# Four of the first seven context loads issued by ScalarE, two small tables loaded later, and another order of the last unit's products

## The chip, the cores and the metric

The kernel runs on one core of a Trainium2 chip. The metric is the time of one execution on the device, in microseconds (us). The engines are TensorE (PE, with its weight loads as PEld), VectorE (DVE), ScalarE (ACT), GpSimd (POOL) and SyncE (SP), which here only issues transfers. Each has its own list of instructions and waits on semaphores that the others raise. 16 DMA engines move the data. In the profile q1 is the queue of SyncE, q10 that of ScalarE, q0 that of GpSimd.

## The reference

Two layers on x (2 batches x 64 positions x 1024) with a context of 2 x 1024 x 1024. Only the very first step matters here, a matmul of x and the context, both rounded to 8-bit codes:

```python
q1 = fake_quant(x1, x1_scale, x1_zp)      # x1 = layernorm(x)
q2 = fake_quant(x2, x2_scale, x2_zp)      # x2 = ctx_4096
...
    q = jnp.clip(jnp.round(x / s + z), QMIN, QMAX)
    return (q - z) * s
...
x = x + jnp.matmul(q1, q2)
x = x + mamba_layer(layernorm(x))         # first product: hidden @ W_in.T
```

Then come a state space layer (`W_in`, convolution, scan, `W_out`), a routed low-rank layer, cross attention on the context, self attention and a small MLP.

## The kernel before

The weights and the context are cut into units of 128 partitions x 2048 float32 (1 MiB, 8 KB per partition). `units` lists them in the order of use: units 0 to 7 are the context, 8 to 23 `w_in`, and so on. They go through a ring of 7 slots; `place(n)` is the slot of unit n, `unit_in[slot]` its semaphore (16 per transfer). SyncE issues x, then all units in order (L516, L533). Unit 7 takes the slot of unit 0 and is issued when unit 0 is coded (`ctx_scaled`, 1), unit 8 when unit 1 is coded. Ahead of unit 12 stand five small loads of the state space layer, `a_par` the last of them.

The context stage, with who does what:
- ScalarE (L675) turns each unit into 8-bit codes as soon as it has landed, 0 to 7 in order; unit 7 in two halves. Between units 1 and 2 it also sums the codes of x (L670).
- VectorE normalizes x, codes it (`q1`), then for each unit takes off 128 and writes bf16 (L1453, `ctx_coded`). Between units 0 and 1 it copies the transposed q1 (L1458), which TensorE's products need.
- TensorE transposes q1 (L931), then for each unit makes four products with q1 (L956) and four with ones (L957, the sums that the zero point needs), in turns. Units 0 to 3 are the first 512 columns of x, 4 to 7 the second. For the second half of unit 7 it waits for `ctx_coded`, 9. After units 3 and 7 it raises `q_done`. Then come 17 idle products (34 matmuls of the trace, L937), which only keep it busy, and the transposes of the next h.
- VectorE, after its last code, adds offset (L1464) and product (L1469) of each half to x, each followed by the statistics for the next layernorm (L1413). GpSimd takes the variance to the power of -0.5 (L558). Then h is written (L1422), transposed, copied by ScalarE and VectorE (L686, L1495), and the products with `w_in` begin (L1017).

At its start GpSimd issues `tables` (72 KB, L546; read first in the self attention near the end) and ScalarE issues `quant` (the four scales, L658) and `tri` (32 KB, L659; read by the routing after the state space layer). After its second variance root GpSimd waits for `q_done`, 2, and clears the edge of `uT` (L587), which VectorE needs before it copies the first projection (L1501). In the scan of the state space layer ScalarE makes 256 exponentials (L768) for 32 steps; at step 26 it issues five loads (L815 to L819).

Of the kernel before, what the change touches and what calls it, by code (L numbers as in the profile page):

```python
# [21 lines left out]
P = 128  # L22
B, L = 2, 64
D = 1024
KT = D // P
UK = 4
UN = 512
UNIT = UK * UN
SPARE = 2
SLOTS = 7  # L30
LN_EPS = 1e-5

# [56 lines left out]
def perceiver(nc, dram, out):  # L89
    units = unit_list()  # L90
# [6 lines left out]
    with ExitStack() as stack:  # L97
# [5 lines left out]

        ring = sb("ring", [P, SLOTS, UNIT])
        x = sb("x", [P, D])
# [3 lines left out]
        small = sb("small", [P, 640])  # L109
# [9 lines left out]
        psum = stack.enter_context(nc.psum_tensor("psum", [P, 8, 512], F32))  # L119
# [54 lines left out]
        tri = carve(small, 528, NE, NE)  # L174


        q2 = arena[:, 0:8192].bitcast(BF16).rearrange("p (u n) -> p u n", u=8)
        q1T = arena[:, 8192:8704].bitcast(BF16).rearrange("p (k t) -> p k t", k=KT)
# [43 lines left out]
        ring_more = carve(arena, 7168, UNIT)  # L222
        ring_spare = carve(arena, 11392, SPARE, UNIT)

# [29 lines left out]

        unit_in = [sem(f"unit_in{s}") for s in range(SLOTS + 2)]
        x_in = sem("x_in")
        quant_in = sem("quant_in")
        tables_in = sem("tables_in")
        tri_in = sem("tri_in")
# [38 lines left out]
        q_done = sem("q_done")  # L298
# [150 lines left out]

        spare = range(first["ctx_again"], first["ctx_again"] + SPARE)  # L450
        before_spare = split_done[sum(n < spare[0] for n in split_units) - 1]
        turns = []
        slot_of = []
# [7 lines left out]
        def place(n):  # L461
            if slot_of[n] > SLOTS:
                return ring_spare[:, slot_of[n] - SLOTS - 1, :]
            return ring_more if slot_of[n] == SLOTS else ring[:, slot_of[n], :]
# [8 lines left out]
        def arrived(eng, n):  # L473
            if n in spare:

                eng.wait_ge(unit_in[SLOTS + 1], 16 * SPARE)
            else:
# [36 lines left out]
        @block.sync  # L514
        def _(sp):
            sp.dma_start(x[:, :], dram["x"]).then_inc(x_in, 16)  # L516
            for n, (name, i) in enumerate(units):
                if n == 12:

                    sp.dma_start(small[:, 320:416], dram["chan"]).then_inc(mamba_in, 16)  # L520
                    sp.dma_start(rms_w, dram["rms_w"].to_broadcast([P, SSM])).then_inc(mamba_in, 16)
                    sp.dma_start(wxT, dram["wx"]).then_inc(mamba_in, 16)
                    sp.dma_start(wdtT[0:R + 1, :], dram["wdt"]).then_inc(mamba_in, 16)
                    sp.dma_start(a_par, dram["a_par"]).then_inc(mamba_in, 16)

                if n == more:
                    sp.wait_ge(y_psum, 2)
                elif n in spare:

                    sp.wait_ge(*before_spare)  # L530
                elif n >= SLOTS:
                    sp.wait_ge(*last_use[before(n)])
                sp.dma_start(place(n), dram[name][i]).then_inc(unit_in[min(slot_of[n], SLOTS + 1)], 16)  # L533

            sp.wait_ge(v_ready, 3)
            sp.dma_start(vdup[L:P, 0, :], vdup[0:L, 0, :]).then_inc(vdup_in, 16)
            sp.dma_start(vdup[0:L, 1, :], vdup[L:P, 1, :]).then_inc(vdup_in, 16)
            for nh in range(2):
                sp.wait_ge(y_ready, nh + 1)
                cols = slice(nh * UN, nh * UN + UN)  # L540
                sp.dma_start(out[:, cols], y_out[:, cols]).then_inc(out_done, 16)
            sp.wait_ge(out_done, 32)

        @block.gpsimd
        def _(pool):
            pool.dma_start(small[:, 160:304], dram["tables"]).then_inc(tables_in, 16)  # L546
            pool.memset(ident[:, :], 0.0).then_inc(const_zero, 1)
            pool.memset(minus_half, -0.5).then_inc(const_zero, 1)
            pool.memset(const_warm, 0.0).then_inc(const_ready, 1)
# [33 lines left out]

            rstd_of(1)

            pool.wait_ge(q_done, 2)
            pool.memset(uT[:, :, :, 0:CK - 1], 0.0).then_inc(edge_zero, 1)  # L587

            pool.wait_ge(ssm_sum, 1)
# [59 lines left out]
        def _(act):  # L649
# [6 lines left out]


            act.dma_start(quant, dram["quant"].to_broadcast([P, 4])).then_inc(quant_in, 16)  # L658
            act.dma_start(tri, dram["tri"]).then_inc(tri_in, 16)  # L659

            act.wait_ge(const_ready, 3)
            step(act.activation(const_warm, const_warm, ACT.Identity))
# [132 lines left out]
            for s in range(3, STEPS):  # L797
                decay(s)
                if s - 1 in Z_AT:
                    softplus_exp(2 + Z_AT.index(s - 1))  # L800
                    softplus_log(2 + Z_AT.index(s - 1))
                if s - 1 in DU_AT:
                    du_copy(DU_AT.index(s - 1) + 1)
                if s == 17:
                    proj_copy(6)
                if s - 1 in GATE_AT:
                    gate_tanh(GATE_AT.index(s - 1))
                if s == 29:
                    proj_copy(7)
                if s == 30:  # L810
                    gated_high(GATE_HALF)
                if s == 26:

                    act.wait_ge(du_copied, NG)
                    act.dma_start(lora_b, dram["lora_b"]).then_inc(rank_in, 16)  # L815
                    act.dma_start(w_ar, dram["w_ar"]).then_inc(rank_in, 16)
                    act.dma_start(b_base, dram["b_base"]).then_inc(bias_in, 16)
                    act.dma_start(bq, dram["bq"].to_broadcast([P, D])).then_inc(bias_in, 16)
                    act.dma_start(bk, dram["bk"].to_broadcast([P, D])).then_inc(bias_in, 16)  # L819
# [61 lines left out]
            for r in range(GQ):  # L881
                last = act.activation(krep[:, :, r, :], krot.rearrange("p (g d) -> p g d", g=HKV), ACT.Copy)
# [3 lines left out]
            for b in range(B):  # L886
                rows = slice(L * b, L * b + L)
# [38 lines left out]
        def _(pe):  # L926
# [17 lines left out]
            for nh in range(2):  # L944
                for kh in range(2):
                    for b in range(B):
                        u = 4 * nh + 2 * kh + b
                        pe.wait_ge(ctx_coded, u + 1)
                        rows = slice(L * b, L * b + L)
                        for k in range(UK):  # L950
                            if u == 7 and k == UK // 2:
                                pe.wait_ge(ctx_coded, 9)
                            right = q2[:, u, UN * k:UN * k + UN]
                            at = dict(start=(kh == 0 and k == 0), stop=(kh == 1 and k == UK - 1))

                            pe.matmul(psum[rows, nh, :], q1T[:, UK * kh + k, rows], right, **at)  # L956
                            last = pe.matmul(psum[rows, 2 + nh, :], ones64, right, **at)  # L957
                last.then_inc(q_done, 1)

            def split_products(bank, left, m, k0, start, stop, signal, hook=None, fresh=None):  # L960

# [233 lines left out]
            for k in range(KT):  # L1195
                last = pe.matmul(psum[:, 2, 0:NE * RANK + NE], hT[:, k, :], w_ar[:, k, :], start=(k == 0), stop=(k == KT - 1))
# [159 lines left out]
            for nh in range(2):  # L1356
                for part, signal in enumerate((hs_high, hs_low)):
                    for k in range(KT):
                        if nh == 0 and k % 4 == 0:
                            pe.wait_ge(signal, 9 + k // 4)  # L1360
                        last = pe.matmul(psum[:, 4 + nh, :], split[:, part, k, :], onehot[:, k, UN * nh:UN * nh + UN],  # L1361
                                         start=(part == 0 and k == 0), stop=(part == 1 and k == KT - 1))
# [8 lines left out]
            for a in range(MH // 2):  # L1371
                pe.wait_ge(g_hi if a >= 4 else g_lo, 1)
                for m in range(2):
                    for r in range(2):
                        rows = slice(MD * r, MD * r + MD)
                        at = 256 * (a % 2) + P * m
                        last = pe.matmul(psum[:, 4 * r + a // 2, at:at + P], up[rows, a, P * m:P * m + P], gT[rows, a, :],
                                         start=True, stop=True)
                if a % 2:
                    last.then_inc(up_psum, 1)  # L1380
            for a in range(MH // 2):
                pe.wait_ge(hidden_ready, 2 * (a // 2 + 1))
                for m in range(2):
                    for r in range(2):
                        last = pe.matmul(psum[MD * r:MD * r + MD, a // 4, P * (a % 4):P * (a % 4) + P], down[:, m, 2 * a + r, :],
                                         hidden[:, 2 * a + r, m, :], start=(m == 0), stop=(m == 1))
                if a % 4 == 3:
                    last.then_inc(down_psum, 1)
            for nh in range(2):
                for part, signal in enumerate((o_high, o_low)):  # L1390
                    for k in range(KT):
                        if nh == 0 and k % 4 == 0:
                            pe.wait_ge(signal, k // 4 + 1)
                        if nh == 0 and part == 0:
                            pe.wait_ge(place_ready, k + 1)
                        last = pe.matmul(psum[:, 2 + nh, :], split[:, part, k, :], onehot[:, k, UN * nh:UN * nh + UN],  # L1396
                                         start=(part == 0 and k == 0), stop=(part == 1 and k == KT - 1))
# [3 lines left out]
        def _(dve):  # L1401
# [7 lines left out]
            def halves(nh):  # L1409
                return slice(UN * nh, UN * nh + UN)  # L1410
# [16 lines left out]
            def x_updated(ins):  # L1427

                ins.then_inc(x_ready, 1)
                updates[0] += 1  # L1430
                dve.wait_ge(x_ready, updates[0])
                statistics((updates[0] - 1) % 2)
# [33 lines left out]

            def context_product(nh):

                x_updated(dve.scalar_tensor_tensor(out=x[:, halves(nh)], in0=psum[:, nh, :], scalar=q_s12,  # L1469
                                                   in1=x[:, halves(nh)], op0=ALU.mult, op1=ALU.add))  # L1470

# [86 lines left out]
            for i, (a, c) in enumerate(parts):  # L1558
                last = dve.tensor_scalar(rms_var[:, i:i + 1], rms_sum[:, i:i + 1], 1.0 / (c - a), RMS_EPS, ALU.mult, ALU.add)
# [359 lines left out]
```

## Time and profile before

| what | value |
|---|---|
| median of 3 runs | 390.81 us (389.24 to 392.25) |
| the profiled execution | 390.28 us, span of the instructions 388.5 us |
| TensorE busy | 356.5 us, 92% of the span |
| VectorE busy | 269.0 us, 69% |
| ScalarE busy | 197.7 us, 51% |
| GpSimd busy | 115.3 us, 30% |
| moved by DMA | 81.34 MB, 209 GB/s on average |
| mean granted clock of TensorE | 0.996 |

The span reaches from the first instruction to the last; the time of an execution is 1.8 us longer. Busy shares are means over stages with different limits, so the chain of waits and the timelines of single stretches tell more.

### The profile page before, as it was taken

The page shows a single profiled execution, that of the slowest core. Times are in us where ns is not written, and L with a number is a line of the kernel's source. Part 1 is how long each engine was busy: PE and PEld are TensorE (multiplying, and loading weights), DVE is VectorE, ACT ScalarE, POOL GpSimd, SP SyncE. Part 2 cuts the span into 40 slices and gives each one's busy share as a digit, 9 for nine tenths or more (in the row PEclk, how much of TensorE's full clock was granted, in tenths as well). Part 3 has the DMA queues.
Part 4 walks back from the last instruction along what each step waited for, and adds up shares of the span by engine and source line. Part 5 has one row for each costly group of instructions (what it writes and reads, how often), then busy time and mean ns, then how long its engine had stood idle before and what let it go on. Part 6 is the DMA issues. An engine that isn't in the chain of part 4 may idle for free.

```text
span 388.5 us, 5274 instructions
## 1 busy us (share of the span) xinstructions
PE 356.5 (92%) x2054; PEld 231.9 (60%) x2054; DVE 269.0 (69%) x334; ACT 197.7 (51%) x397; POOL 115.3 (30%) x97
## 2 busy tenths in 40 slices
PE   0788999999999999999999999899999989999996
PEld 0335444653566666556655777688343567788785
DVE  2757057757887999998973777786820788975281
ACT  1980133169999697677710744463021279251160
POOL 2600000024999798889910000002000000310000
PEclk9999999999999999999999989999999999999999
DMA  6999999553002020254128798299999995000001
GB/s 251 423 424 392 352 420 345 213 197 128 2 3 109 0 90 19 94 189 156 56 108 283 272 412 349 93 347 345 365 422 401 416 426 214 2 2 2 0 2 54
DMA packets 12825, 81.34 MB, mean 209 GB/s; under 512 B 2094, under 2 KB 2350, under 8 KB 3519
## 3 DMA queue, kind: packets, MB, share of 16 engines
q1 hardware_dynamic: 11614, 78.23, 52.4%
q10 hardware_dynamic: 1154, 2.70, 2.1%
q8 instruction: 16, 0.26, 0.3%
q14 instruction: 9, 0.07, 0.1%
q0 software_dynamic: 32, 0.07, 0.0%
HBM read 80.34 MB, written 0.52 MB: 208 GB/s over the span
## 4 chain that ended last, share of the span: by engine, by line
PE 57%; DVE 16%; POOL 11%; issue 7%; DMA 6%; ACT 3%; POOLq 0%; SPq 0%; DVEq 0%; ACTq 0%
PE psum L1017 10%; PE psum L969 9%; PE psum L1137 7%; PE psum L1242 6%; DMA ring<-in_ctx 6%; PE psum L1093 5%; POOL arena L618 5%; PE psum L976 4%; PE psum L931 3%; PE psum L1161 3%; DVE arena L1595 2%; POOL arena L621 2%; PE psum L1361 2%; PE psum L1396 2%; POOL plain L618 2%
## 5 line engine op out<-in xcount | busy, mean ns | idle before, releaser
L768 ACT ACTIVATE arena<-arena 128x126 f32<-128x126 f32 x256 | 76.5, 387 | 9.7 <-DVE arena L1595 9.2
L1017 PE MATMUL psum<-ring,hT 128*128 128x512 f32 x128 | 60.7, 603 | 0.8 <-ACT hT L686 0.8
L1595 DVE TENSOR_TENSOR_SCAN arena<-arena,psum 128x1024 f32<-128x1024 f32 x24 | 54.2, 2273 | 3.2 <-PE psum L1093 3.0
L618 POOL TENSOR_TENSOR arena<-arena 128x1024 f32<-128x1024 f32 x20 | 47.2, 2359 | 5.4 <-DVE arena L1595 5.4
L1137 PEld LDWEIGHTS psum<-arena,ident 128*128 128x128 f32 x292 | 35.6, 192 | 13.8 <-issue 9.2
L1638 DVE TENSOR_TENSOR rounded<-ring,rounded 128x2048 fp32r<-128x2048 f32 x16 | 36.4, 2284 | 9.9 <-ACT rounded L795 9.9
L795 ACT ACTIVATE rounded<-ring 128x2048 fp32r<-128x2048 f32 x16 | 30.6, 1914 | 24.1 <-PE psum L976 14.7
L558 POOL TENSOR_TENSOR small<-small 128x1 f32<-128x1 f32 x6 | 3.3, 554 | 124.2 <-DVE small L1419 124.2
L1137 PE MATMUL psum<-arena,ident 128*128 128x128 f32 x292 | 37.3, 278 | 1.6 <-POOL arena L621 1.6
L1017 PEld LDWEIGHTS psum<-ring,hT 128*128 128x128 f32 x128 | 22.2, 190 | 27.1 <-issue 26.0
L1093 PE MATMUL psum<-plain 64*128 64x512 f32 x128 | 36.1, 641 | 1.7 <-DVE arena L1595 1.3
L969 PE MATMUL psum<-rounded,split 128*128 128x512 f32 x96 | 25.1, 405 | 1.2 <-DVE rounded L1638 0.9
L1242 PE MATMUL psum<-ring,arena 128*64 128x512 f32 x96 | 24.4, 593 | 0.0
L931 PE MATMUL psum<-ident,h 128*128 128x128 f32 x48 | 8.3, 329 | 14.7 <-DVE h L1446 11.8
L937 PEld LDWEIGHTS psum<-ident 128*128 128x128 f32 x160 | 19.2, 192 | 4.4 <-issue 4.0
L931 PEld LDWEIGHTS psum<-ident,arena 128*128 128x128 f32 x120 | 13.4, 140 | 13.8 <-issue 7.3
L969 PEld LDWEIGHTS psum<-rounded,split 128*128 128x128 f32 x96 | 18.0, 193 | 6.0 <-issue 1.0
L621 POOL TENSOR_TENSOR arena<-arena 128x256 f32<-128x256 f32 x23 | 21.0, 915 | 1.6
L937 PE MATMUL psum<-ident 128*128 128x128 f32 x160 | 21.4, 283 | 0.0
L931 PE MATMUL psum<-ident,arena 128*128 128x128 f32 x120 | 18.7, 280 | 2.9 <-POOL arena L600 0.9
L1595 DVE TENSOR_TENSOR_SCAN plain<-arena,psum 128x1024 f32<-128x1024 f32 x8 | 18.2, 2272 | 4.1 <-PE psum L1093 4.1
L675 ACT ACTIVATE arena<-ring,small 128x2048 uint8<-128x2048 f32 (+1 forms) x9 | 16.9, 1900 | 8.1 <-DMA ring<-in_ctx 8.1
(209 smaller groups left out, 584.6 us busy)
## 6 DMA issues: line engine op xcount, KB each, us to landing
ring<-in_w_in SPq DMA_DIRECT2D x16, 1024.0 KB, 12.7
ring<-in_ctx SPq DMA_DIRECT2D x13, 1024.0 KB, 12.1
ring<-in_w_out SPq DMA_DIRECT2D x8, 1024.0 KB, 4.8
ring<-in_ctx_t SPq DMA_DIRECT2D x7, 1024.0 KB, 6.1
ring<-in_w_base SPq DMA_DIRECT2D x4, 1024.0 KB, 4.8
ring<-in_x_wk SPq DMA_DIRECT2D x4, 1024.0 KB, 6.5
ring<-in_a_wo SPq DMA_DIRECT2D x4, 1024.0 KB, 11.4
ring<-in_x_wq SPq DMA_DIRECT2D x3, 1024.0 KB, 8.9
```

Of the source, the lines that this page charges most:

```text
L618: pool.tensor_tensor(state[s % STATES], state[s % STATES], c, ALU.mult).then_inc(prod_ready, 1)
L768: last = act.activation(to, of, ACT.Exp, scale=a_par[:, k, state_no:state_no + 1])
L795: act.activation(unit_halves[m % 3][:, 0, :, :], slot(split_units[m]), ACT.Copy).then_inc(unit_high, 1)
L931: last = pe.transpose(psum[:, bank, P * k:P * k + P], tile[:, c:c + P], ident[:, :])
L937: pe.matmul(psum[:, bank, 0:P], ident[:, :], ident[:, :], start=True, stop=True)
L969: pe.matmul(psum[:, bank, :], left(0, k0 + k), unit[:, w, k, :], start=(start and k == 0 and w == 0), stop=False)
L1017: last = pe.matmul(psum[:, proj_bank(j), :], hT[:, k, :], slot(w_in + u)[:, k % UK, :], start=(k == 0), stop=(k == KT - 1))
L1093: last = pe.matmul(psum[:, input_bank(s, b), :], du[rows_of(b), left], bdiag[rows_of(b), right, :], start=True, stop=True)
L1137: last = pe.matmul(psum[:, 6 + g % 2, cols], ident[:, :], v[:, n, :, :], start=(s % 2 == 0 and n == 0), stop=(s % 2 == 1 and n == count - 1))
L1242: last = pe.matmul(psum[L * b:L * b + L, bank, :], left[:, UK * kh + k, L * b:L * b + L], slot(u0 + b)[:, k, :], start=(kh == 0 and k == 0 ...
L1595: dve.tensor_tensor_scan(state[s % STATES], dA[:, s % 3, :], psum[:, p:p + 2, :].rearrange("p a b -> p (a b)"), 0.0, ALU.mult, ALU.add).th ...
L1638: dve.tensor_tensor(unit[:, 1, :, :], slot(split_units[m]), unit[:, 0, :, :].bitcast(F32), ALU.subtract).then_inc(unit_low, 1)
```

## The change

ScalarE issues units 0, 2, 4 and 6 behind `quant`; SyncE skips them and issues x, 1, 3, 5, 7, 8, and so on, with the same waits as before. The load of `tables` moves behind GpSimd's second variance root, that of `tri` to step 26 of the scan, ahead of `lora_b`. On TensorE the products of unit 7 with ones come first and raise `q_done` to 2; its four products with q1 follow and raise it to 3. VectorE waits for 3 ahead of the second half's product, GpSimd ahead of the memset of `uT`.

```diff
+ACT_LOADS = (0, 2, 4, 6)
...
             for n, (name, i) in enumerate(units):
+                if n in ACT_LOADS:
+                    continue
...
         def _(pool):
-            pool.dma_start(small[:, 160:304], dram["tables"]).then_inc(tables_in, 16)
...
             rstd_of(1)
 
-            pool.wait_ge(q_done, 2)
+            pool.dma_start(small[:, 160:304], dram["tables"]).then_inc(tables_in, 16)
+            pool.wait_ge(q_done, 3)
             pool.memset(uT[:, :, :, 0:CK - 1], 0.0).then_inc(edge_zero, 1)
...
             act.dma_start(quant, dram["quant"].to_broadcast([P, 4])).then_inc(quant_in, 16)
-            act.dma_start(tri, dram["tri"]).then_inc(tri_in, 16)
+            for n in ACT_LOADS:
+                act.dma_start(place(n), dram[units[n][0]][units[n][1]]).then_inc(unit_in[slot_of[n]], 16)
...
                     act.wait_ge(du_copied, NG)
+                    act.dma_start(tri, dram["tri"]).then_inc(tri_in, 16)
                     act.dma_start(lora_b, dram["lora_b"]).then_inc(rank_in, 16)
...
-                            pe.matmul(psum[rows, nh, :], q1T[:, UK * kh + k, rows], right, **at)
+                            if u < 7:
+                                pe.matmul(psum[rows, nh, :], q1T[:, UK * kh + k, rows], right, **at)
                             last = pe.matmul(psum[rows, 2 + nh, :], ones64, right, **at)
                 last.then_inc(q_done, 1)
+            for k in range(UK):
+                last = pe.matmul(psum[L:P, 1, :], q1T[:, UK + k, L:P], q2[:, 7, UN * k:UN * k + UN], start=False, stop=(k == UK - 1))
+            last.then_inc(q_done, 1)
...
             def context_product(nh):
 
+                if nh:
+                    dve.wait_ge(q_done, 3)
```

## Rows read from the trace of the kernel before

**Rows 1.** Chain that ended last, by time: start us, us, what

```profile
11.47 15.20 DMA ring<-in_ctx
...
37.80 8.82 PE psum L1017 x20
```

**Rows 2.** Timeline of ScalarE, 0 to 38 us: start us, us, instruction [idle before, releaser]

```profile
1.65 1.28 ACT L664 ACT_TABLE_LOAD   x1 [1.65 <-PEq L1912]
...
9.35 2.10 ACT L675 ACTIVATE arena<-ring,small 128x2048 uint8<-128x2048 f32 x1 [6.20 <-DMA ring<-in_ctx]
11.78 2.10 ACT L675 ACTIVATE arena<-ring,small 128x2048 uint8<-128x2048 f32 x1 [0.33 <-DMA ring<-in_ctx]
13.78 1.04 ACT L670 ACTIVATE arena<-h 128x1024 f32<-128x1024 f32 x1
...
14.81 4.07 ACT L675 ACTIVATE arena<-ring,small 128x2048 uint8<-128x2048 f32 x2
...
26.69 2.37 ACT L675 ACTIVATE arena<-ring,small 128x1024 uint8<-128x1024 f32 x2 [0.38 <-DMA ring<-in_ctx]
```

**Rows 3.** DMA queues, 9.5 to 26 us: packets, MB, share of 16 engines

```profile
q1 hardware_dynamic: 963, 6.99, 101.5%
```

**Rows 4.** Line 533, 0 to 60 us: issues of context units, ns min/median/max, first and last start

```profile
L533 SPq DMA_DIRECT2D ring<-in_ctx x8: 327/509/707, 1.2 to 11.5; - x8
```

**Rows 5.** Timeline of VectorE, 9 to 38 us

```profile
11.65 1.22 DVE L1453 TENSOR_SCALAR arena<-arena 128x2048 bf16<-128x2048 uint8 x1
...
13.79 0.69 DVE L1458 CAST arena<-psum 128x512 bf16<-128x512 f32 x1 [0.16 <-PE psum L931]
...
29.10 0.69 DVE L1453 TENSOR_SCALAR arena<-arena 128x1024 bf16<-128x1024 uint8 x1 [0.44 <-ACT arena L675]
...
31.88 0.73 DVE L1464 SCALAR_TENSOR_TENSOR x<-psum,small,x 128x512 f32<-128x512 f32 x1
32.66 0.75 DVE L1469 SCALAR_TENSOR_TENSOR x<-psum,small,x 128x512 f32<-128x512 f32 x1
```

**Rows 6.** Timeline of TensorE's matmuls, 11 to 39 us

```profile
14.54 0.64 PE L956 MATMUL psum<-arena 128*64 128x512 bf16 x1 [0.78 <-DVE arena L1458]
14.97 0.63 PE L957 MATMUL psum<-arena 128*64 128x512 bf16 x1
...
20.13 0.38 PE L956 MATMUL psum<-arena 128*64 128x512 bf16 x1
20.34 0.38 PE L957 MATMUL psum<-arena 128*64 128x512 bf16 x1
...
30.52 0.38 PE L957 MATMUL psum<-arena 128*64 128x512 bf16 x1
30.83 4.06 PE L937 MATMUL psum<-ident 128*128 128x128 f32 x34
35.86 1.11 PE L931 MATMUL psum<-ident,h 128*128 128x128 f32 x8 [0.97 <-DVE h L1422]
```

**Rows 7.** DMA queues, 6 to 7 us

```profile
q1 hardware_dynamic: 45, 0.36, 85.0%
...
q10 hardware_dynamic: 46, 0.01, 5.0%
```

**Rows 8.** DMA queues, 5 to 9.5 us

```profile
q0 software_dynamic: 32, 0.07, 4.2%
q10 hardware_dynamic: 179, 0.03, 3.8%
```

**Rows 9.** Windows: PE, PEld, DVE, ACT, POOL busy (instructions), PEclk, DMA share, GB/s

```profile
14.00:20.00 6.00, 5.46 (x20) 2.62 (x21) 4.25 (x4) 5.64 (x5) 4.07 (x3) 1.00 1.02 423
```

**Rows 10.** Timeline from the start, all engines: GpSimd's load

```profile
1.24 0.78 POOL L546 DMA_DIRECT2D small<-in_tables  x1 [0.80 <-POOLq L1912]
```

**Rows 11.** Timeline of VectorE, 34 to 48 us

```profile
47.16 0.69 DVE L1501 COPY arena<-psum 128x512 f32<-128x512 f32 x1 [2.04 <-PE psum L931]
```

**Rows 12.** Timeline of ScalarE, 155 to 200 us

```profile
175.04 4.76 ACT L768 ACTIVATE arena<-arena 128x126 f32<-128x126 f32 x16 [2.31 <-DVE arena L1595]
```

## The prediction

> **What bounds the kernel now.** I read the chain of waits first, in order of time. From 11.47 to 26.67 us it is one single piece of 15.20 us, the transfer of context units [rows 1]. From 37.80 us on TensorE's products with `w_in` carry the chain. So the stage that the change touches is bound by when the units land, and by what ScalarE, VectorE and TensorE still have to do after the last of them. ScalarE's own timeline says the same: it sits idle for 6.20 us until unit 0 is there at 9.35, codes a unit in 2.1 us, and then waits 0.3 to 0.4 us for nearly every further one [rows 2]; from 11.78 to the start of unit 7 at 26.69 there are six steps, 2.49 us each. The queue view gives the reason: between 9.5 and 26 us the SyncE queue alone fills all 16 DMA engines (101.5%, 6.99 MB) [rows 3]. A megabyte at that rate takes 1.049 / 6.99 x 16.5 = 2.48 us. The issue itself takes SyncE 0.33 to 0.71 us per unit [rows 4]: SyncE issues a unit several times faster than the engines can move it, so its issuing is no bound.
>
> The second thing to see is what follows the last landing. Unit 7 is coded in two halves: ScalarE from 26.69 for 2.37 us, to 29.06 [rows 2]; VectorE turns the second half from 29.10 and then goes without a pause through offset and product of both halves of x (31.88 and 32.66 are those of the second half) [rows 5]. TensorE's last context product starts at 30.52 [rows 6], 1.4 us ahead of the VectorE operation that reads the second half's sums, at 31.88.
>
> **Part 1: ScalarE issues units 0, 2, 4, 6; SyncE issues x, 1, 3, 5, 7.** The four issues cost ScalarE at most 4 x 0.71 = 2.8 us [rows 4], less the one of `tri` that goes. Its activation table load starts at 1.65 and takes 1.28 [rows 2]; even 2.8 us later all of it is over by 6 us, and ScalarE now idles until 9.35. Cost: none.
>
> What changes is the order in which the units land. The number of bytes up to the end of unit 7 doesn't, as they still pass the same 16 full engines [rows 3]. With work on two queues, how do they share? The trace has a case of it: while unit 0 moves on SyncE's queue, `tri` moves on ScalarE's. From 6 to 7 us the first did 45 packets and the second 46 [rows 7], and in the 4.5 us from 5 us on the second has 179 with 0.03 MB in all [rows 8]. Had the engines served its queue in one go, `tri` (32 KB) would have been gone in a small part of a microsecond. Instead it is stretched over the whole time of unit 0: the engines take packets of the two queues in turn, one for one, whatever their size. Units are all alike (128 packets of 8 KB), x and `quant` have 128 packets each too, so the two queues stay abreast: units 0 and 1 land together, then 2 and 3, 4 and 5, 6 and 7. Each pair lands when its second unit lands now. Unit 7 is issued once unit 0 is coded, some 12 us ahead of its data, so SyncE's queue has no hole.
>
> Now the sum. The tables (queue 0) and `tri` (in queue 10) no longer move ahead of the context: 4.2% and at most 3.8% of 4.5 us [rows 8] are 0.19 + 0.17 us; as `quant` is part of the latter, I take 0.32 us. The last pair is then there for ScalarE at 26.69 - 0.32 = 26.37. ScalarE can't have coded unit 6 by then, as it now does; it must code unit 6 (4.07 / 2 = 2.03 us) and unit 7 (2.37) behind that point [rows 2]: 26.37 + 2.03 + 2.37 = 30.77, against 29.06. If unit 6 lands one packet of 0.31 us ahead of unit 7 it is 30.46. The loss is 1.4 to 1.7 us; I take 1.6. Checking that ScalarE isn't later still: unit 0 starts at 11.78 - 0.32 = 11.46 at the latest, units 0 and 1 are coded by 15.6, the sum of q1 (13.78 to 14.81 now, 1.03 us) by 16.6, units 2 and 3 by 20.7; units 4 and 5 land at 11.46 + 4 x 2.48 = 21.4 and are coded by 25.5, so unit 6 does wait for its data. Everything behind it on VectorE's line moves by the same 1.6 us, as that line has no gap from 29.10 on.
>
> **Part 2: TensorE.** Now unit 0 is turned by VectorE at 11.65, then q1T is copied until 14.48 [rows 5], and products start at 14.54 [rows 6]. As the turn of unit 0 stands ahead of the copies in VectorE's order, this becomes 11.46 + 2.10 + 1.22 + 2 x 0.69 = 16.2. The products then go at a start-to-start step of 0.43 us, later of 0.21 us [rows 6]; the change between them comes at 19.8 to 20.1, after 13 products. The granted clock reads 1.00, the 2.4 GHz level, from 14 to 20 us too [rows 9], so the rows of the clock don't tell the two paces apart and I use the steps alone. After the change: 13 products at 0.43 end at 21.8, then TensorE catches up with the codes (8 x 0.215 = 1.7 us a unit); unit 6 is coded at 28.4 + 1.22 = 29.6, its 8 products end at 31.3 and those of unit 7 at 33.0. VectorE wants the second product half at 32.66 + 1.6 = 34.3. Hidden by 1.2 us.
>
> **Part 3: offset products first, with a signal of their own.** The eight matmuls of unit 7 are the same in another order: four with ones, then four with q1. The first signal comes 4 x 0.21 = 0.86 us sooner, but it has no customer: the offset operation at 31.88 is queued behind three others on VectorE, while TensorE is done at 30.52 + 0.38 = 30.9 [rows 5, 6]. Gain 0. The price: ahead of the wait for the second half of the codes only two matmuls can run instead of four, which would make the last product 2 x 0.21 = 0.43 us later if TensorE stood waiting there; by part 2 it is behind at that point, and the order costs nothing. After unit 7 come the 34 filler matmuls (4.06 us) [rows 6]: they end at 33.1 + 4.06 = 37.2, the transposes of h are wanted at 35.86 + 1.6 = 37.5. Cover of 0.3 us, against 0.97 now; I take 0 and allow 0.5 us in the range. VectorE's new wait stands ahead of one operation only and is met by then.
>
> **Part 4: moved loads.** The tables are issued on GpSimd behind the second variance root, 0.78 us [rows 10], ahead of a wait and the memset of uT's edge. VectorE needs that edge before its copy at 47.16, which waits for TensorE [rows 11]: some 10 us of cover; without it the cost is 0.8 us. The new wait (third signal instead of second) makes GpSimd wait 0.9 us longer, under the same cover. The 72 KB then share the engines with `w_in`, 0.2 us, and TensorE doesn't wait for a `w_in` unit in its 20 products from 37.80 [rows 1]. `tri` costs ScalarE one issue (0.33 to 0.71 us) at step 26 of the scan, ahead of `lora_b`; ScalarE then has 2.31 us idle at 175.04, waiting for VectorE [rows 12]. Zero. At the start nothing waits for GpSimd's earlier memsets, so that gains nothing.
>
> **Sum.** -0.3 (bytes gone) and +1.9 (unit 6 coded behind the last landing) = +1.6 us. On the profiled execution (390.28 us, span 388.5) 391.9; that execution lies 0.53 us below the median of 390.81, so the median should go to 392.4. Nothing behind takes it back: from 37.80 on the chain is work of the engines, and SyncE's later issues wait for that work, so they move along.
>
> **Rivals.** (A) The engines serve one queue for a whole unit before turning to the other, ScalarE's first. Then units land in today's order at today's pace, and only the 0.32 us stays: 390.5 as median, faster by 0.1%. Against it: the even packet counts [rows 7]. Where SyncE's queue goes first, unit 6 is still the last to land, and the loss stays 1.6 us. The Trainium skill ("DMA: Bandwidth & Descriptors", section on queues, rings and completion order) speaks for A: an engine drains a whole packet, typically 9 to 17 descriptors, from one ring before it switches. By that rule the rows of `tri` would not look as they do. Chance of A 0.12.
> (B) Slower by more: TensorE becomes the bound. It starts 1.7 us later behind a longer pause (it waits 0.78 us ahead of 14.54 now [rows 6], 2.4 us then), and if it stays at the 0.43 us step longer than now, its backlog reaches the end. Without any wait its 64 products end at 16.2 + 64 x 0.215 + n x 0.215 = 30.0 + 0.215 n, n being those at the slow step; the cover ends at 33.3, so it decides from n = 16, with 13 seen now. At n = 20, a slow stretch of 8.6 us, it costs 0.9 us more; with four units slow (n = 32) 3.5 us: 395.9. Chance 0.10.
> (C) Two queues fill the engines sooner at the start. x and unit 0, 1.57 MB, take until 9.35 [rows 2], where at the rate of rows 3 they would need 3.7 us; of that gap up to 2 us could come back and leave -0.3 + 1.9 - 2.0 = -0.4 us, 390.4. But x and `quant` stand first on both queues as they do now. I count it in the range, with 0.03.
>
> **How the numbers follow.** Forecast 0.75, A 0.12, B 0.10, C 0.03. Repeated runs of one kernel spread by 3 us here (389.24 to 392.25), so under 1%, 3.9 us, is about what can't be told from no change. The forecast, A and C lie within it; of B about half is beyond. Some chance on either side is for what I don't see: faster 0.03, same 0.91, slower 0.06. The range goes from rival A less 1.2 us of spread, 389.3, to the forecast with the 0.9 us of B and 1.3 us of spread, 394.6.
>
> **What would show it.** Right: ScalarE starts unit 0 at about 11.3, units in pairs back to back with waits only ahead of 2k; last code ends near 30.7 us; VectorE's second product at 34.3; first `w_in` product at 39.4; from there the traces run parallel. Rival A: unit 0 codes at 9.1. B: TensorE's filler ends after h is ready, and transposes follow it without idle time. The prediction is wrong as a whole if the units don't land in pairs, or if the shift of 1.6 us at the first `w_in` product isn't there at the end.

## The result, and the profile after

The changed kernel takes 391.62 us as the median of 20 runs (391.18 to 392.96), the kernel before 389.46 (389.24 to 392.25, 20 runs): ratio 1.0045, 95% interval 1.0034 to 1.0057, so 1.3 to 2.2 us slower (the medians themselves differ by 2.16). The time stated ahead of the prediction, 390.81, was the median of the first three of those 20.

The profile of the changed kernel shows the loss whole, before 40 us. ScalarE's timeline, the answer to [rows 2]:

```profile
11.74 4.08 ACT L677 ACTIVATE arena<-ring,small 128x2048 uint8<-128x2048 f32 x2 [6.57 <-DMA ring<-in_ctx]
15.72 1.04 ACT L672 ACTIVATE arena<-h 128x1024 f32<-128x1024 f32 x1
...
16.76 4.06 ACT L677 ACTIVATE arena<-ring,small 128x2048 uint8<-128x2048 f32 x2
21.59 4.08 ACT L677 ACTIVATE arena<-ring,small 128x2048 uint8<-128x2048 f32 x2 [0.76 <-DMA ring<-in_ctx]
26.57 4.36 ACT L677 ACTIVATE arena<-ring,small 128x2048 uint8<-128x2048 f32 x3 [0.90 <-DMA ring<-in_ctx]
```

Units are coded two at a time (x2, at the end x3, as unit 7 has two halves), and ScalarE waits only ahead of a pair. It waits for unit 6 until 26.57 and codes 6 and 7 behind it, until 30.93; before, only unit 7 was left at 26.69 and the end was 29.06. The queue views of 6 to 7 us and of 9.5 to 26 us answer to [rows 7] and [rows 3]:

```profile
q10 hardware_dynamic: 32, 0.22, 52.4%
q1 hardware_dynamic: 27, 0.21, 50.3%
```

```profile
q1 hardware_dynamic: 502, 3.60, 52.1%
q10 hardware_dynamic: 474, 3.38, 49.0%
```

Each queue has half of the engines, and the total of the view is the same 6.99 MB in 16.5 us as before: here two queues move nothing faster. Behind the last code, VectorE (answer to [rows 5]):

```profile
13.86 1.23 DVE L1460 TENSOR_SCALAR arena<-arena 128x2048 bf16<-128x2048 uint8 x1 [2.18 <-ACT arena L677]
15.01 1.28 DVE L1465 CAST arena<-psum 128x512 bf16<-128x512 f32 x2
...
30.95 0.69 DVE L1460 TENSOR_SCALAR arena<-arena 128x1024 bf16<-128x1024 uint8 x1 [0.43 <-ACT arena L677]
...
33.74 0.73 DVE L1471 SCALAR_TENSOR_TENSOR x<-psum,small,x 128x512 f32<-128x512 f32 x1
34.51 0.75 DVE L1478 SCALAR_TENSOR_TENSOR x<-psum,small,x 128x512 f32<-128x512 f32 x1
```

The offset operation of the second half (L1471) starts 1.86 us later than before, although TensorE's signal for it is now a separate and earlier one. TensorE's matmuls (answer to [rows 6]):

```profile
16.34 0.63 PE L960 MATMUL psum<-arena 128*64 128x512 bf16 x1 [2.65 <-DVE arena L1465]
...
29.97 0.40 PE L960 MATMUL psum<-arena 128*64 128x512 bf16 x1 [1.08 <-DVE arena L1460]
...
32.16 1.03 PE L964 MATMUL psum<-arena 128*64 128x512 bf16 x4
33.11 4.06 PE L940 MATMUL psum<-ident 128*128 128x128 f32 x34
37.71 1.11 PE L934 MATMUL psum<-ident,h 128*128 128x128 f32 x8 [0.54 <-DVE h L1429]
39.65 8.82 PE L1024 MATMUL psum<-ring,hT 128*128 128x512 f32 x20 [0.83 <-ACT hT L688]
```

The first product with `w_in` starts at 39.65 instead of 37.80 [rows 1]: +1.85 us. Matched one by one, TensorE's matmuls then stay 1.85 to 1.94 us late up to 224 us. The span of this execution is 391.2 against 388.5. Another 0.5 us of the 2.7 comes between 224 and 233 us, where the granted clock falls in both kernels, and the last 0.3 us comes in small steps behind 300 us. The windows of the first of these stretches, before and after (columns as in [rows 9]):

```profile
222.00:229.00 7.00, 7.00 (x26) 4.77 (x25) 4.50 (x9) 4.01 (x5) 0.55 (x1) 0.76 0.91 343
```

```profile
224.00:231.00 7.00, 7.00 (x27) 4.76 (x26) 4.00 (x9) 3.50 (x5) 0.55 (x1) 0.76 0.89 345
```

The profiled execution of the changed kernel (392.96 us) is the longest of its 20. The timed runs are the better measure, and the shift of the first product, 1.85 us, lies in their interval of 1.3 to 2.2.

### The profile page after: what moved, and what is told of

Its sections match the earlier page's. It is cut to its first block, busy times and chain, and to the rows that moved or that the text cites. A ratio compares the mean times of both kernels' runs of the same rounds, so it can differ in the third digit from the quotient of the medians.

```text
span 391.2 us, 5275 instructions
## 1 busy us (share of the span) xinstructions
PE 356.5 (91%) x2054; PEld 231.8 (59%) x2054; DVE 268.8 (69%) x334; ACT 197.4 (50%) x397; POOL 114.6 (29%) x97
## 4 chain that ended last, share of the span: by engine, by line
PE 53%; DVE 15%; POOL 11%; DMA 10%; issue 7%; ACT 3%; ACTq 1%; POOLq 0%; DVEq 0%
PE psum L1024 10%; PE psum L976 9%; PE psum L1144 7%; DMA ring<-in_ctx 6%; PE psum L1100 5%; POOL arena L621 5%; PE psum L983 4%; PE psum L1249 4%; DMA ring<-in_a_wkv 4%; PE psum L1168 3%; PE psum L934 3%; DVE arena L1604 2%; POOL arena L624 2%; PE psum L1368 2%; PE psum L1403 2%
## 5 line engine op out<-in xcount | busy, mean ns | idle before, releaser
L934 PEld LDWEIGHTS psum<-ident,arena 128*128 128x128 f32 x120 | 13.4, 140 | 13.9 <-issue 7.3
```

The costliest lines, as they stand in the source:

```text
L934: last = pe.transpose(psum[:, bank, P * k:P * k + P], tile[:, c:c + P], ident[:, :])
```

## The experiments

Twelve kernels ran, each beside the kernel before. The second column is the end of ScalarE's last code, the third the start of the first `w_in` product, both in the profiled execution (us); the medians and the ratio are of the timed runs. The fifth column is the median of the kernel before in the runs beside this kernel, which the ratio refers to.

| kernel | last code | first w_in | median us | before beside it | ratio (95%) |
|---|---|---|---|---|---|
| before | 29.06 | 37.80 | 389.46 | - | 1 |
| changed | 30.93 | 39.65 | 391.62 | 389.46 | 1.0045 (1.0034 to 1.0057) |
| loads_only | 31.17 | 39.90 | 391.88 | 389.75 | 1.0061 (1.0040 to 1.0082) |
| tri_ahead | 32.03 | 40.77 | 392.74 | 389.75 | 1.0073 (1.0049 to 1.0098) |
| no_split | 28.55 | 37.29 | 389.08 | 389.75 | 0.9976 (0.9955 to 0.9996) |
| three_loads | 29.94 | 38.68 | 390.77 | 389.75 | 1.0020 (1.0003 to 1.0037) |
| products_only | 28.99 | 37.73 | 389.65 | 389.66 | 0.9998 (0.9983 to 1.0013) |
| load_0 | 29.02 | 37.76 | 389.76 | 389.66 | 0.9997 (0.9977 to 1.0017) |
| load_6 | 30.06 | 38.81 | 390.88 | 389.66 | 1.0025 (1.0006 to 1.0043) |
| quant_behind_x | 29.82 | 38.56 | 390.15 | 389.66 | 1.0010 (0.9994 to 1.0027) |
| quant_rows | 29.13 | 37.86 | 389.69 | 389.39 | 0.9998 (0.9978 to 1.0018) |
| quant_in_x | 26.53 | 35.27 | 386.94 | 390.15 | 0.9919 (0.9906 to 0.9931) |
| quant_in_x_halves | 26.18 | 34.91 | 387.13 | 390.15 | 0.9924 (0.9910 to 0.9939) |
| quant_in_x_four_loads | 28.16 | 36.90 | 388.24 | 390.15 | 0.9953 (0.9939 to 0.9967) |

The third column less the second is 8.72 to 8.75 us in all fourteen: whatever a kernel does to the context stage reaches the rest only by the end of the last code. These two columns have one execution each, but are sharp: products_only, which changes nothing ahead of the last code, ends it 0.07 us from the kernel before. The ratios settle only what is above half a microsecond or so.

**loads_only.** One part of the change alone, `tri` behind the units:

```diff
             act.dma_start(quant, ...).then_inc(quant_in, 16)
+            for n in ACT_LOADS:
+                act.dma_start(place(n), dram[units[n][0]][units[n][1]]).then_inc(unit_in[slot_of[n]], 16)
             act.dma_start(tri, dram["tri"]).then_inc(tri_in, 16)
```

> The kernel before with one part of the change: ScalarE issues units 0, 2, 4, 6 behind quant, and tri behind them. The tables stay at the start, TensorE's order stays. Theory (packets of the two queues in turn, so units land in pairs and unit 6 lands last): the loss of the change without the 0.17 us of tri still behind the units and with the 0.19 us of the tables added back, ScalarE's last code ends at about 31.1 us against 29.06, time +2.0 us (ratio 1.005). Rival 1 (the loss comes from TensorE's new order and its signal): no loss here, within 0.3 us of before. Rival 2 (the loss comes from ScalarE's late first unit, whatever the pairs): about the same +2.0, told apart by the kernel with three loads.

Last code at 31.17, ratio 1.0061. The loss is that of the loads; rival 1 falls. Rival 2 is left to three_loads and load_0.

**tri_ahead.** The same with the `tri` line ahead of the loop.

> As loads_only, but tri stays ahead of the four units on ScalarE's queue. Theory (one packet each in turn, whatever the size): the 8 packets of tri per engine pass in turn with the 8 packets of unit 1, so ScalarE's queue falls behind by one whole unit: unit 1 lands alone, then 0 with 3, 2 with 5, 4 with 7, and unit 6 with the first w_in unit, 2.5 us later than in loads_only. Last code at about 33.5 us, time +4.4 us against before (ratio 1.011). Rival (the queues share by bytes, or a whole unit at a time): 32 KB more or less in front cost under 0.2 us, same time as loads_only.

The turns are there. ScalarE's timeline and, from 7 to 9 us, the queues:

```profile
14.72 4.08 ACT L680 ACTIVATE arena<-ring,small 128x2048 uint8<-128x2048 f32 x2 [9.06 <-DMA ring<-in_ctx]
...
19.75 12.28 ACT L680 ACTIVATE arena<-ring,small 128x2048 uint8<-128x2048 f32 x7
```

```profile
q1 hardware_dynamic: 98, 0.67, 79.6%
q10 hardware_dynamic: 101, 0.13, 18.1%
```

98 packets against 101, though q1 moves 0.67 MB and q10 0.13: turns go by packets, not by bytes. Unit 0 is 14.72 - 11.98 = 2.7 us later than in loads_only (one unit, 2.48 us, and a little) for 32 KB put in front of it. The end I got wrong: 32.03, not 33.5. From 14.72 on ScalarE never waits, and its own 17.3 us of work set the end. It would have waited if unit 6 had come 2.5 us later than in loads_only, at 29.3, as expected; unit 6 landed at 27.6, just ahead of its turn. The expectation overlooked that SyncE issues unit 7 only when unit 0 is coded, here at 16.8. So SyncE's queue ran dry, and from 18 to 20 us ScalarE's queue had all engines and caught up:

```profile
q10 hardware_dynamic: 112, 0.85, 101.9%
q1 hardware_dynamic: 4, 0.00, 0.1%
```

The measured time doesn't tell this kernel from loads_only (the intervals overlap).

**no_split.** The changed kernel with `ACT_LOADS = ()`.

> The changed kernel with all context units issued by SyncE again; tables and tri late and TensorE's new order stay. Theory: only the 0.3 us of the removed bytes is left: last code at 28.75, time -0.3 us against before (ratio 0.999). Rival (TensorE's new order costs its 0.43 us or more): time +0.1 us or more.

ScalarE codes unit 7 from

```profile
26.18 2.37 ACT L677 ACTIVATE arena<-ring,small 128x1024 uint8<-128x1024 f32 x2 [0.39 <-DMA ring<-in_ctx]
```

0.51 us sooner than before, rather than 0.3. So the removed loads were worth 0.5 us, and the four loads on ScalarE cost 30.93 - 28.55 = 2.38 us. The rest of the change is a gain, of 0.2 to 1.8 us by the ratio.

**products_only.** TensorE's order and the third signal alone:

```diff
+                            if u < 7:
+                                pe.matmul(psum[rows, nh, :], q1T[...], right, **at)
                             last = pe.matmul(psum[rows, 2 + nh, :], ones64, right, **at)
                 last.then_inc(q_done, 1)
+            for k in range(UK):
+                last = pe.matmul(psum[L:P, 1, :], q1T[:, UK + k, L:P], q2[:, 7, ...], ...)
+            last.then_inc(q_done, 1)
```

> The kernel before with TensorE's new order of unit 7 and the new signal alone. Theory: the last product is up to 0.43 us later (start at 30.95 instead of 30.52), the fillers end at 35.3, still ahead of the transposes of h at 35.86; VectorE's offset operation of the second half stays at 31.9. Time within 0.2 us of before. Rival (the new signal lets VectorE go on earlier): offset operation before 31.8 and a gain. Rival (the longer work behind the last code is seen): transposes later than 35.9.

```profile
30.23 1.03 PE L961 MATMUL psum<-arena 128*64 128x512 bf16 x4
31.19 4.06 PE L937 MATMUL psum<-ident 128*128 128x128 f32 x34
35.79 1.11 PE L931 MATMUL psum<-ident,h 128*128 128x128 f32 x8 [0.54 <-DVE h L1426]
```

The fillers (the 34 idle matmuls) start 0.36 us later (30.83 in [rows 6]), and 0.43 us later counted from the end of the last code, which is 0.07 us sooner here. TensorE's idle time ahead of the transposes is 0.54 instead of 0.97, and nothing else moves. VectorE's offset operation starts at 31.81, the ratio is 0.9998. Neither a gain nor a loss is seen; the interval leaves room for some 0.6 us either way.

**three_loads.** `ACT_LOADS = (0, 2, 4)`.

> The changed kernel with ScalarE issuing only units 0, 2, 4; unit 6 stays with SyncE. Theory: three pairs, but then units 6 and 7 land one after the other on SyncE's queue, and ScalarE codes unit 6 while unit 7 moves: last code at 28.75, time -0.3 us against before, though the first unit is as late as in the changed kernel (11.7 us) and TensorE starts at 16.3. Rival (the loss comes from the late first unit, from ScalarE's or TensorE's later start): a loss of 1 us or more stays.

Missed: 29.94, not 28.75.

```profile
21.61 8.33 ACT L677 ACTIVATE arena<-ring,small 128x2048 uint8<-128x2048 f32 x5 [0.78 <-DMA ring<-in_ctx]
```

Unit 6 does land ahead of unit 7, but ScalarE is still at units 4 and 5 then, which came together at 21.6. It has four units to code behind that point (3 x 2.03 + 2.37 = 8.5 us, 8.33 in the row) and makes up only 2.48 - 2.03 = 0.45 us per unit. The theory needed a second part: each late landing leaves a bound "landing of unit n, then all codes from n on without a wait", and the latest of these bounds is the end. For the changed kernel that is unit 6, for three_loads unit 4.

**load_0 and load_6.** `ACT_LOADS = (0,)` and `(6,)`, both to test that second part.

> The changed kernel with ScalarE issuing unit 0 alone. The run with three loads kept a loss of 0.9 us, so the theory is corrected by ScalarE's own pace: it codes a unit in 2.03 us while one lands every 2.48, so it makes up only 0.45 us per unit after a pair. For one pair at the start: unit 0 coded from 11.7, sum of q1 behind unit 1, then units 2 to 7 without a wait: 11.7 + 4.05 + 1.03 + 5 x 2.03 + 2.37 = 29.3 as the end of the last code, against 28.55 with no load on ScalarE and 29.94 with three. Rival (the loss grows with the number of ScalarE's loads, or starts only with the last pair): 28.6, or 28.9.

> The changed kernel with ScalarE issuing unit 6 alone, which then passes in turn with unit 0 and lands at 11.5. Corrected theory (landing and ScalarE's pace together): units 1 to 5 land 2.48 us apart from 13.7 on, unit 5 at 23.7, and units 5, 6, 7 are all coded behind 23.9: 23.9 + 2 x 2.03 + 2.37 = 30.4 as the end of the last code, 1.8 us more than with no load, although unit 6 was there 12 us ahead. Rival (only a late unit 6 costs): 28.6.

```profile
16.73 12.29 ACT L677 ACTIVATE arena<-ring,small 128x2048 uint8<-128x2048 f32 x7
```

```profile
23.72 6.34 ACT L677 ACTIVATE arena<-ring,small 128x2048 uint8<-128x2048 f32 x4 [0.40 <-DMA ring<-in_ctx]
```

Ends of 29.02 and 30.06, where 29.3 and 30.4 were expected (my 2.03 and 2.37 us each hold a little that overlaps). In load_6 the row also starts 0.2 us sooner than expected. One pair at the start costs 0.5 us against no_split. This answers rival 2 of loads_only: the first code starts as late in load_0 (11.71) as in the changed kernel (11.74), yet the loss is 0.5 and not 2.4 us. A unit 6 that is there 12 us ahead costs 1.5 us: it took its share of the engines from the units that were needed first, and unit 5 was left for the end together with 6 and 7.

**quant_behind_x.** With the theory settled, the question was what does bound this stage. Its start is slow: x and unit 0 take until 9.35 us [rows 2]. The edit moves `quant` to SyncE, behind x, on no_split.

> The kernel no_split with quant issued by SyncE behind x, so that nothing passes in turn with x. From 2 to 5.5 us the engines moved x at half of the full rate while the 128 packets of quant (16 B) passed in turn with it. Theory A (each small packet costs an engine some 0.2 us, wherever it stands): x lands about 1.5 us sooner, unit 0 at the same time, last code 28.5, no gain. Theory B (the start is slow because of latency, and quant hides in it): x lands sooner, quant and unit 0 within 0.3 us of no_split. Theory C (only passing in turn with x makes quant slow): unit 0 lands 1 us sooner, last code 27.6, time -0.9 us against no_split.

Windows of its start (last two columns: share of the DMA engines, GB/s):

```profile
2.00:3.00 1.00, 0.00 (x0) 0.00 (x0) 0.00 (x0) 0.21 (x2) 0.00 (x0) 1.00 0.84 299
3.00:4.00 1.00, 0.00 (x0) 0.00 (x0) 0.00 (x0) 0.00 (x0) 0.00 (x0) 1.00 0.45 177
4.00:5.00 1.00, 0.00 (x0) 0.00 (x0) 0.00 (x0) 0.00 (x0) 0.00 (x0) 1.00 0.57 58
```

x is there 3.3 us after its issue, against 5.5 in no_split, and then the engines move almost nothing for a microsecond and a half: `quant`, 2 KB, takes 4.9 us from its issue. Last code at 29.82, 1.3 us later than in no_split. That is worse than each of the three theories; C is out. A, small packets that hold the engines, fits best, as in front of the units they do so with nothing else to move beside them; but this run alone doesn't tell A from B, latency at the start; quant_in_x does.

**quant_in_x.** The scales become four more columns of x, repeated for each partition on the host, where the kernel's layouts are made; the arithmetic is unchanged.

```diff
-        x = sb("x", [P, D])
+        x_quant = sb("x_quant", [P, D + 4])
+        x = x_quant[:, 0:D]
+        quant = x_quant[:, D:D + 4]
...
-            sp.dma_start(x[:, :], dram["x"]).then_inc(x_in, 16)
+            sp.dma_start(x_quant[:, :], dram["x_quant"]).then_inc(x_in, 16)
...
-            act.dma_start(quant, dram["quant"].to_broadcast([P, 4])).then_inc(quant_in, 16)
```

> The kernel no_split with the four scales as four more columns of x: one load of 128 x 1028 on SyncE, no load of quant. The run quant_behind_x had x landed at 3.9 us and quant 2.1 us later though it holds 2 KB, and unit 0 behind it. Theory (each of quant's 128 small packets holds an engine for 0.2 us or more): these 2 us go; x lands at 4 us, unit 0 at 6.5, all units 2 us sooner than in no_split, last code 26.5 against 28.55, time -2 us against no_split and about -2.7 against before (ratio 0.993). Rival (the first 2 us of any transfer are slow, whatever is moved): x lands at 4, but unit 0 not before 8, gain under 0.5 us against no_split. Rival (ScalarE or VectorE become the bound): unit 7 waits in the ring, gain between.

```profile
3.00:4.00 1.00, 0.00 (x0) 0.00 (x0) 0.00 (x0) 0.00 (x0) 0.00 (x0) 1.00 1.12 464
4.00:5.00 1.00, 0.00 (x0) 0.00 (x0) 0.89 (x3) 0.00 (x0) 0.00 (x0) 1.00 0.94 377
```

```profile
6.80 2.09 ACT L676 ACTIVATE arena<-ring,x_quant,small 128x2048 uint8<-128x2048 f32 x1 [4.57 <-DMA ring<-in_ctx]
...
24.16 2.37 ACT L676 ACTIVATE arena<-ring,x_quant,small 128x1024 uint8<-128x1024 f32 x2 [0.40 <-DMA ring<-in_ctx]
```

The engines run at 377 to 464 GB/s from 3 us on, so B, latency at the start, is out too. Unit 0 is coded from 6.80 instead of 9.35 and the last code ends at 26.53: 2.5 us ahead of the kernel before. The time is 386.94 us, ratio 0.9919 (2.7 to 3.7 us): the fastest kernel of this study, and faster than both. The kernel before has a median of 390.15 over the nine runs beside it; against the 389.46 of its 20 runs the gain is 2.5 us, as the last code says. The chain is still the context: one piece of 15.2 us.

**quant_in_x_halves.** Unit 7 in two transfers on top of that:

```diff
+                if n == 7:
+                    first_half, last_half = code_parts(n)
+                    sp.dma_start(place(n)[:, first_half], dram[name][i][:, first_half]).then_inc(half_in, 16)
+                    sp.dma_start(place(n)[:, last_half], dram[name][i][:, last_half]).then_inc(unit_in[slot_of[n]], 16)
+                    continue
```

> As quant_in_x, with unit 7 loaded in two halves (two transfers of 4 KB rows, a semaphore each), so that ScalarE codes the first half while the second moves. ScalarE is busy with unit 6 until about 23.7 and waits for unit 7 until 24.1 in quant_in_x: the gain is bounded by that 0.4 us. Last code 26.1, time -0.4 us against quant_in_x, hardly measurable. Rival (a second completion, or 4 KB packets, cost something): no gain.

The last code ends 0.35 us sooner, as expected; the time (387.13, ratio 0.9924) doesn't show it. Inconclusive.

**quant_in_x_four_loads.** The changed kernel with the scales in x's load.

> The changed kernel (ScalarE issues 0, 2, 4, 6) with the scales in x's load. ScalarE's queue now has nothing in front of unit 0, so it is ahead by one: unit 0 passes in turn with x, 2 with 1, 4 with 3, 6 with 5, and unit 7 moves alone. Theory of turns of one packet: x lands later than in quant_in_x (5.7 us) with unit 0, units 1 and 2 at 10.7, 3 and 4 at 15.7, 5 and 6 at 20.9, 7 at 23.6; ScalarE, with 2.03 us a unit, ends the last code at 27.5 to 27.9 against 26.5, a loss of 1.2 us against quant_in_x and not of the 2.4 us that the four loads cost in the changed kernel. Rival (the four loads cost 2.4 us in themselves): last code at 28.9.

```profile
7.18 2.09 ACT L676 ACTIVATE arena<-ring,x_quant,small 128x2048 uint8<-128x2048 f32 x1 [2.86 <-DVE small L1445]
11.88 2.09 ACT L676 ACTIVATE arena<-ring,x_quant,small 128x2048 uint8<-128x2048 f32 x1 [2.61 <-DMA ring<-in_ctx]
...
14.91 6.10 ACT L676 ACTIVATE arena<-ring,x_quant,small 128x2048 uint8<-128x2048 f32 x3
21.82 6.34 ACT L676 ACTIVATE arena<-ring,x_quant,small 128x2048 uint8<-128x2048 f32 x4 [0.80 <-DMA ring<-in_ctx]
```

The groups are now unit 0 alone (with x), 1 and 2, 3 and 4, and the last wait is the one for unit 5, at 21.82. That is the order that turns of one packet give when ScalarE's queue has nothing in front of unit 0. The first code waits for VectorE, which needs x: x and unit 0 share the engines, and x comes at 6.9 us, not at the 5.7 that I had expected. The loss against quant_in_x is 28.16 - 26.53 = 1.6 us: more than my 1.2 by 0.4, and less than the 2.4 of the same four loads behind `quant`. Which units share the engines follows from what stands ahead of them on each queue.

**quant_rows.** As quant_behind_x, with `quant` stored as 128 rows of 16 B:

```diff
-            sp.dma_start(quant, dram["quant"].to_broadcast([P, 4])).then_inc(quant_in, 16)
+            sp.dma_start(quant, dram["quant"]).then_inc(quant_in, 16)
```

> As quant_behind_x, but quant lies in memory as 128 rows of 16 B, one for each partition, instead of one row that all 128 packets read. The packets keep their size and number. Theory A (reading one and the same 16 B 128 times is what holds the engines): quant is through 0.3 us after x (4.3 us), last code near 26.8, about 3 us sooner than in quant_behind_x. Theory B (packets of 16 B are slow wherever they read): x at 3.9, quant at 6.0, last code 29.8 as in quant_behind_x.

```profile
3.00:4.00 1.00, 0.00 (x0) 0.00 (x0) 0.00 (x0) 0.00 (x0) 0.00 (x0) 1.00 0.91 305
4.00:5.00 1.00, 0.00 (x0) 0.00 (x0) 0.82 (x3) 0.00 (x0) 0.00 (x0) 1.00 0.81 279
6.00:7.00 1.00, 0.00 (x0) 0.00 (x0) 0.30 (x1) 0.00 (x0) 0.89 (x4) 1.00 0.97 295
```

With the same packets but 128 addresses the hole of quant_behind_x is gone (279 GB/s from 4 to 5 us, where it had 58), and `quant` is there 3.0 us after its issue instead of 4.9: it is the reading of one and the same 16 B that makes this load slow. But half of the forecast failed: the engines stay near 300 GB/s until 7 us instead of 420, unit 0 is coded from 9.46, and the last code ends at 29.13, not 26.8: only 0.7 us sooner than in quant_behind_x, and 2.6 us later than in quant_in_x. From 6 to 7 us the engines are busy, with 36 packets of 8 KB in 97% of their time: 0.43 us each, where one takes 0.31 us at the 424 GB/s of the view of 9.5 to 26 us. It isn't a matter of this one execution: the ten timed runs take 389.04 to 391.24 us, the five of quant_in_x 386.76 to 386.98. What slows unit 0 stays open, and with it why a separate load costs more than the time in which it is read.

## Why the prediction was right

The forecast was 392.4 us with 389.3 to 394.6, +1.6 us; measured were 391.62 and, by the ratio, +1.3 to +2.2 us. The direction and the mechanism held. The size held in part by luck, as two errors of the sum cancel in part.

- **Bound of the stage.** Right. The last code's end carries over to the first `w_in` product without change in all fourteen kernels.
- **Part 1, landing in pairs.** Right, and told from its rivals by tri_ahead and quant_in_x_four_loads. The view of [rows 7], 45 packets against 46, was the row that decided it. Rival A (a whole unit per turn) is out: with both queues full of units, 32 and 27 packets go in the same microsecond, and units are coded in pairs. Unit 0 lands a little after unit 1 here: SyncE's queue was ahead by a packet or two. So ScalarE starts unit 0 at 11.74, where the prediction had 11.46 at the latest.
- **Its sum.** The two terms were each too small, and the errors partly cancel. Bytes gone: 0.3 said, 0.5 measured (no_split). Units 6 and 7 behind the last landing: 1.9 said, 2.4 measured. Of these 2.4, unit 6's code is 4.36 - 2.37 = 2.0, as said. The other 0.4 is a term that the prediction had at nothing: it took two queues to bring the eighth unit at the same time as one, and ScalarE's last wait ends at 26.57 instead of 26.18 in no_split. Unit 7, issued at 13.9, landed 12.1 us later, at 25.9; unit 6, issued at 3.0, landed 23.5 us later, at 26.5. SyncE's queue was done with the context first and moved parts of `w_in` while unit 6 was still under way. Total +1.6 said, +1.85 seen at the first `w_in` product. The forecast for unit 6's start was 26.37 and it was 26.57; the last code was to end at 30.77 and ended at 30.93.
- **Part 2, TensorE.** Start of the products 16.2 said, 16.34 measured, the fast step from 21.5 (21.8 said). The prediction took the 1.00 of [rows 9] for the granted clock of the slow step too. But the trace's clock record has its first entry at 20.0 us before and at 21.3 after, and the view shows 1.00 where there is none. The step shortens at 20.1 and 21.5, so the record begins where the step changes and says nothing on the clock of the slow step. I had TensorE busy with a backlog at unit 7; in fact it had caught up and waited 1.08 us for unit 6's code. The fillers' start of 33.1 was right all the same. Rival B didn't occur.
- **Part 3, the new order.** Right that it gains nothing and costs nothing; wrong in the reason why the order adds no delay. It does add 0.4 us (products_only: 0.36, and 0.43 counted from the last code, which is the price that the prediction named and then took at nothing), which the idle time ahead of the transposes takes up: 0.54 us left, 0.3 said.
- **Part 4.** Right. The tables' issue and the memset end at 38.2 us, the copy that needs the memset comes at 49.0.
- **Rival C.** Right that the start of both queues would not get faster, but its cause is not what I had in mind. Most of those 2 us could be had: not with two queues, but by taking `quant`'s 128 packets away (last code 28.55 to 26.53).

The median of before that the absolute time was built on (390.81 of three runs) lay 1.35 us above that of 20. For that reason the measured time lies 0.8 us below the absolute forecast; on the median of 20 the forecast would have been 391.1, 0.6 us too low.

## What to carry to other kernels

Ask first whether issuing is the bound; here SyncE issued a unit in 0.33 to 0.71 us and the engines took 2.48. As the transfers already filled the DMA engines, a second queue added no rate and changed the order of landing: two units shared the engines and both landed at about the time of the second. A consumer that takes units one by one wants them one by one, the last above all; its cost is found by asking, for every unit, "landing, plus all the consumer's work from there on", and taking the latest. Look at the first microseconds for small loads that repeat one row for all partitions: 2 KB of scales cost this kernel 2.0 us (last code at 28.55 with them and at 26.53 without), as much as the whole change. Putting them into the load of x gave that back; storing them as 128 rows of their own did not (29.13).

## What I had not expected of the hardware

- The turns between two queues went by packets whatever their size: 98 packets (0.67 MB) against 101 (0.13 MB) from 7 to 9 us in tri_ahead. So 32 KB in front of a unit held it back by 2.7 us against loads_only. The Trainium skill ("DMA: Bandwidth & Descriptors", queues, rings and completion order) says that a DMA engine drains a packet of typically 9 to 17 descriptors from one ring before it switches. No run here shows turns that long: in those 2 us the profile has 98 pieces of one queue and 101 of the other, which is about 6 of each for each of the 16 engines.
- 128 packets that all read the same 16 B kept the 16 engines from other work for about 1.5 us (58 GB/s from 4 to 5 us in quant_behind_x) and landed 4.9 us after their issue. With 128 separate rows of 16 B the hole is gone (279 GB/s) and the load takes 3.0 us; yet the last code ended only 0.7 us sooner, for a reason that stays open.
- The granted clock of TensorE, at its 2.4 GHz level nearly everywhere, falls in some executions near 225 us, with TensorE busy throughout both before and in it (7.00 of 7 us): the mean over the 7 us is 0.76, and from 225 to 228 us of the kernel before it reads 0.50, the 1.2 GHz level. The profiled executions of before, changed, three_loads, tri_ahead, products_only and quant_in_x_halves have it (mean clock 0.995 or 0.996), the others don't (0.999 or 1.000). The changed kernel's runs with a mean clock of 0.999 or 1.0 lie at 391.2 to 391.8 us, those with 0.995 or 0.996 at 391.9 to 393.0. So for this kernel it goes with most of the spread that I had put down as noise. It is also why shifts at the first `w_in` product and shifts of the whole differ: TensorE's matmuls in quant_in_x are 2.5 us ahead of the profiled execution of the kernel before up to 224 us and 3.4 us ahead from 231 on, those in no_split 0.5 and 1.4, as that execution has the fall and these two don't. For the kernel before only the profiled execution has its clock on record, so how often its other runs had it isn't shown. Nor is what sets it off.
